# A block's preparation rebuilt, and D/2 added to the score tile by GpSimd instead of by matmuls

## The chip, the cores and the metric

The kernel runs on one core of one Trainium2 chip, in one launch. The metric is the time of that launch on the device, in microseconds. The core has five engines that matter here: TensorE (PE; its weight loads are PEld), VectorE (DVE), ScalarE (ACT), GpSimd (POOL) and SyncE (SP), which only issues DMAs. TensorE runs at one of two clocks, 1.2 or 2.4 GHz, and the profile tells which was granted as a share of the full one.

## The reference, cut to what matters

The input is two images of 64 by 64 positions with 64 channels. Four stages each add to it; the last two hold four bidirectional "mamba2" blocks each, along rows and along columns in turn. There are thus eight blocks, one after another, and these are what the change touches:

```python
def _mamba2(x, Win, Wconv, bconv, dt_bias, A_log, D, gn_w, Wout):
    z = zxbcdt[..., :DIN]
    xBC = jax.nn.silu(_causal_conv(zxbcdt[..., DIN:DIN + CONVDIM], Wconv, bconv))
    dt = jax.nn.softplus(zxbcdt[..., -NHEADS:] + dt_bias)
    A = -jnp.exp(A_log)
    y = _ssd(xh, dt, A, Bm, Cm) + rev(_ssd(rev(xh), rev(dt), A, rev(Bm), rev(Cm)))
    y = y + D[None, None, :, None] * xh
    y = _rmsnorm(y.reshape(b, l, DIN) * jax.nn.silu(z), gn_w)
    return y @ Wout
```

Its input is `_rmsnorm(x)`, and its output is added to x. `_ssd` forms for every sequence, head and pair of positions the product of a score (C times B), a decay (an exponential of sums of dt times A) and dt, and multiplies the 64 by 64 matrix by the sequence's x. The two directions together are one matrix whose entry is score times the smaller of two exponents' exponential, and D is added on its diagonal.

## The kernel before, in words

The program is written by hand for each engine, with a semaphore for every hand-over (`pe.wait_ge(sg("mixed"), ...)` waits, `.then_inc` tells). Each engine runs its instructions in order. Tokens are kept as 128 partitions (2 images by 64 channels) by 4096 columns, in eight chunks or groups of 512. Eight calls of `call(m, n, d, c)` make the eight blocks, c from 0 to 7; d is 0 for one axis (then a group of 512 columns is read from Y with a stride) and 1 for the other.

A call has three parts.

**Preparation.** ACT squares Y (line 750), PE multiplies by a matrix of 1/64 to get the mean over channels on all 128 partitions (line 476), ACT takes Ln and Exp chunk by chunk (lines 753, 755), and DVE scales Y by it into XP (line 1150). From XP PE makes sixteen chunks of z (line 487; ACT's tanh at line 765 and DVE's multiplication at line 1168 finish them, over four banks) and the chunk of dt (line 495). DVE adds the bias (line 1155), ACT and DVE make the softplus (`softplus_exp`, lines 629 to 635, and `softplus`, line 1005 on), and DVE scans dt times A (line 1179). Four tiles F, E, P, Q of exponents are each split into three bf16 parts: F and E on GpSimd (lines 850 to 853), P and Q on DVE (lines 1160 to 1163). SP stores F's and E's parts to DRAM (line 272) and, group by group, loads rows of them (line 258) and rows of P and Q (line 263). The z chunks and this chain are interleaved on DVE.

**The loop of steps.** `for tau in range(FIRST, LAST)` is run by PE, ACT and DVE, and GpSimd loops over u. Each of the 64 steps u handles one position of the outer axis: PE makes two tiles of exponents (`decay_logs`, lines 550 and 554), ACT copies one out of PSUM (line 780), DVE takes the smaller (line 1249), ACT its exponential (line 774), GpSimd multiplies it by the scores (line 861), and PE multiplies the result with x (`y`, line 570). `y` has 16 matmuls in a step: eight by the constant `Dhalf` (D/2 on a diagonal), eight by the product tile. Around this, with a period of four steps, `project_x` (line 515), ACT's tanh of x (786), `gate_x` (two DVE operations, line 1201) and `gate_y` (line 1231) run; with a period of eight steps `project_bc` (528), `gate_b` and `gate_c` (1213, 1218), `scores` (536), `scale_scores` (1225), ACT's squares (801), `sum_squares` (581), ACT's Ln and Exp of the gate (806, 808), `project_out` (587) and `grow` (1237, 1240). `every(tau, period, offset, count)` fixes the step at which each is placed. DK has three buffers, MM two.

**Tail.** The last output group leaves the loop, and line 1259 tells the next call that Y is ready.

```python
                    for hd in range(2):
                        for by, first_ in ((Dhalf, True), (MM[u % 2], False)):
                            for h4 in range(4):
```

Of the kernel before, what the change touches and what calls it, by code (L numbers as in the profile page):

```python
# [13 lines left out]
ALU = mybir.AluOpType  # L14
ACT = mybir.ActivationFunctionType
# [22 lines left out]
              ("restart", 512), ("dec_rhs", 512), ("dec_lhs", 128), ("thirds", 3), ("two", 1), ("mask16", 16), ("maskbc", 16), ("ones", 128), ("eps6", 1), ("eps6x4", 1), ("eps5", 1),  # L38
# [23 lines left out]
def program(nc, x, consts, pool_sel, state_sel, l0w, l1w, callw, out):  # L62
    ctx = ExitStack()
    with ctx:  # L64
# [83 lines left out]
        tz = [SQ[:, 512 * i:512 * i + 512] for i in range(4)]  # L148
        DT, dte, dtr, dty = (O[:, 512 * i:512 * i + 512] for i in range(4))
        dA_, dF, dE, dL = (O[:, 2048 + 512 * i:2560 + 512 * i] for i in range(4))  # L150
        dP, dQ, rest_v, rest_p = (SQ[:, 2048 + 512 * i:2560 + 512 * i] for i in range(4))

# [53 lines left out]
        LAST, FIRST = L + 15, -9  # L206
# [19 lines left out]
        def _(sp):  # L226
# [11 lines left out]
            def call(m, n, d, c):  # L238
# [12 lines left out]
                def rows_of_decay(g):  # L251
# [3 lines left out]
                    for k, name in enumerate("PQ"):  # L255
                        for j in range(3):
                            r0 = 32 * k + 2 * j
                            sp.dma_start(RHS[g % 2][r0:r0 + 2, :], cols_dram[k, j, 16 * g:16 * g + 16, :].rearrange(
                                "(b h) n -> b (h n)", h=8)).then_inc(sg(f"decay_cols{g % 2}"), 16)
                            l0 = 32 * k + 6 + 8 * j  # L260
                            for b in range(NB):
# [3 lines left out]
                                    sg(f"decay_rows{g % 2}"), 16)  # L265

                rows_of_x(0)
                rows_of_x(1)
                sp.wait_ge(sg("split_p"), c + 1)
                for k, name in enumerate("FE"):  # L270
                    for j in range(3):
                        sp.dma_start(cols_dram[k, j], SPLIT[name][j]).then_inc(sg("decay_stored"), 16)
                sp.wait_ge(sg("split_v"), c + 1)
                sp.wait_ge(sg("decay_stored"), (c + 1) * 96)
                sp.wait_ge(sg("zeroed"), 1)
# [24 lines left out]
        def _(pe):  # L300
# [167 lines left out]
            def call(m, n, d, c):  # L468
# [5 lines left out]
                for ch in range(NCHUNK):  # L474
                    pe.wait_ge(sg("squared"), c * NCHUNK + (ch + 1))
                    mm(bank[ch], C("mean64"), SQ[:, BANK * ch:BANK * ch + BANK], start=True,
                       stop=True).then_inc(sg("norm_ms"), 1)
                pe.wait_ge(sg(f"block_weights_loaded{d}"), (m * 2 + n) * 16 + 16)

                def z(i):  # L480

                    if i >= 4:
                        pe.wait_ge(sg("z_ready"), c * 16 + (i - 3))
                    else:
                        pe.wait_ge(sg("norm_log"), c * NCHUNK + (i + 1))
                        pe.wait_ge(sg("normed"), c * NCHUNK + (i // 2 + 1))
                    mm(bank[i % 4], W(f"wz{i % 2}"), xn_group(i // 2), start=True, stop=True).then_inc(  # L487
                        sg("z_psum"), 1)
                for i in range(4):
                    z(i)  # L490
# [963 lines left out]
```

## Time and profile before

| what | value |
|---|---|
| median of 3 runs | 2945.92 us (2945.87 to 2956.25) |
| the profiled execution's own time | 2958.37 us |
| its span | 2956.6 us |
| TensorE's granted clock, mean | 0.855 |
| PE busy | 2222.7 us, 75% |
| VectorE busy | 1883.0 us, 64% |
| ScalarE busy | 1841.8 us, 62% |
| GpSimd busy | 1088.8 us, 37% |
| the eight calls | from about 902 us to 2934 us |

Busy times are unions of an engine's instructions. They overlap between engines, so they show how full an engine is and not what ends last. The time before 902 us belongs to the first two stages, which the change doesn't touch.

### The profile page before, as it was taken

What the parts mean: (1) busy time and instruction counts of PE and PEld (TensorE: products, weight loads), DVE (VectorE), ACT (ScalarE), POOL (GpSimd) and SP (SyncE); (2) the same over time, 40 slices, a digit from 0 to 9 for tenths busy, and PEclk for the clock granted to TensorE, in tenths of its full rate; (3) what the DMA queues carried; (4) which work ended last, traced back from release to release, by engine and by line L of the source; (5) the groups of instructions that cost most, each with busy time, mean ns of one, the idle gap of its engine ahead of it and who ended that gap; (6) DMA issues with size and microseconds to landing.
All of it is one profiled execution on the core that took longest, in us unless ns stands there. A gap on an engine that the chain in (4) does not pass through costs nothing. (4 is left out here: it accounts for less than half of the span.)

```text
span 2956.6 us, 64250 instructions
## 1 busy us (share of the span) xinstructions
PE 2222.7 (75%) x26182; PEld 1131.4 (38%) x26182; DVE 1883.0 (64%) x2667; ACT 1841.8 (62%) x2939; POOL 1088.8 (37%) x859
## 2 busy tenths in 40 slices
PE   4276776777774897798698679658968986986896
PEld 3022222222221553454255245325524542552553
DVE  2588888888886564664665565566556646666564
ACT  1266766767655666576576657557665764666674
POOL 0044444444442452344154244214414432451342
PEclk6588888888887898898799899779988988998897
DMA  4000000000001111110111011011101101110111
GB/s 132 0 0 1 0 1 0 1 0 0 1 0 27 36 34 26 35 35 13 40 42 25 26 46 34 14 30 42 25 26 42 36 15 40 35 23 26 36 35 30
DMA packets 96695, 74.50 MB, mean 25 GB/s; under 512 B 69392, under 2 KB 77584, under 8 KB 95120
## 3 DMA queue, kind: packets, MB, share of 16 engines
q1 hardware_dynamic: 96400, 70.39, 10.0%
q8 instruction: 206, 3.38, 0.5%
q14 instruction: 89, 0.73, 0.1%
HBM read 20.54 MB, written 8.39 MB: 10 GB/s over the span
## 5 line engine op out<-in xcount | busy, mean ns | idle before, releaser
L861 POOL TENSOR_TENSOR SQ<-SQ 128x512 f32<-128x512 f32 x344 | 449.0, 1307 | 623.9 <-PE bank L570 397.1
L826 POOL TENSOR_TENSOR Y<-Z 128x512 f32<-128x512 f32 x256 | 331.0, 1293 | 530.8 <-DVE Z L1065 297.6
L1249 DVE TENSOR_TENSOR SQ<-bank,O 128x512 f32<-128x512 f32 x344 | 237.2, 690 | 420.0 <-ACT O L780 322.6
L774 ACT ACTIVATE SQ<-SQ 128x512 f32<-128x512 f32 x344 | 215.3, 626 | 202.0 <-DVE SQ L1249 201.9
L780 ACT ACTIVATE O<-bank 128x512 f32<-128x512 f32 x512 | 298.3, 583 | 61.3 <-PE bank L550 59.6
L550 PE MATMUL bank<-SS,work 32*128 32x512 bf16 x512 | 205.3, 401 | 155.8 <-ACT O L780 143.0
L861 POOL TENSOR_TENSOR SQ<-O,SQ 128x512 f32<-128x512 f32 x168 | 221.4, 1318 | 245.4 <-PE bank L570 212.9
L1065 DVE TENSOR_TENSOR_SCAN Z<-bank,SS 128x512 f32<-128x512 f32 x256 | 311.0, 1215 | 0.5
L448 PE MATMUL bank<-Y,constants 128*128 128x512 f32 x512 | 295.2, 661 | 6.5 <-DVE bank L1073 4.8
L515 PE MATMUL bank<-folded_weights,work 128*64 128x128 f32 x4096 | 298.2, 292 | 0.0
L570 PE MATMUL bank<-folded_weights,work 128*32 128x64 f32 x8192 | 283.3, 228 | 13.4 <-POOL SQ L861 13.3
L570 PE MATMUL bank<-SQ,work 128*32 128x64 f32 x8192 | 272.1, 222 | 0.0
L515 PEld LDWEIGHTS bank<-folded_weights,work 128*64 128x64 f32 x4096 | 235.8, 145 | 83.0 <-issue 83.0
L570 PEld LDWEIGHTS bank<-folded_weights,work 128*32 128x32 f32 x8192 | 186.2, 111 | 208.5 <-issue 182.4
L487 PE MATMUL bank<-XP,block_weights 128*128 128x512 f32 x256 | 151.6, 713 | 116.0 <-DVE Z L1168 114.7
L1057 DVE TENSOR_TENSOR SS<-SS,bank 128x512 f32<-128x512 f32 x256 | 173.6, 683 | 82.6 <-PE bank L436 66.9
L1249 DVE TENSOR_TENSOR O<-bank,O 128x512 f32<-128x512 f32 x168 | 115.8, 689 | 167.3 <-ACT O L780 140.9
L554 PE MATMUL bank<-SS,work 32*128 32x512 bf16 x512 | 206.2, 403 | 0.0
L712 ACT ACTIVATE Z<-bank 128x512 f32<-128x512 f32 x256 | 150.9, 590 | 77.7 <-PE bank L440 76.3
L570 PEld LDWEIGHTS bank<-SQ,work 128*32 128x32 f32 x8192 | 196.1, 112 | 0.0
L1201 DVE SCALAR_TENSOR_TENSOR work<-SQ,bank 64x512 f32<-64x512 f32 x256 | 174.3, 681 | 2.3 <-ACT SQ L786 0.3
L440 PE MATMUL bank<-work,Z 96*128 96x512 bf16 x256 | 109.7, 429 | 86.9 <-ACT Z L712 86.6
(260 smaller groups left out, 4064.3 us busy)
## 6 DMA issues: line engine op xcount, KB each, us to landing
work<-XP SPq DMA_DIRECT2D x256, 134.0 KB, 2.4
work<-extra SPq DMA_DIRECT2D x768, 8.0 KB
decay_cols_kept<-extra SPq DMA_DIRECT2D x48, 128.0 KB, 1.8
SS<-decay_cols_kept SPq DMA_DIRECT2D x384, 16.0 KB
block_weights<-callw SPq DMA_DIRECT2D x8, 735.0 KB, 4.2
Z<-state_sel SPq DMA_DIRECT2D x1, 2048.0 KB, 13.2
out<-O SPq DMA_DIRECT2D x2, 1024.0 KB, 8.5
constants<-consts SPq DMA_DIRECT2D x1, 1267.5 KB, 5.9
```

The source lines that it names most:

```text
L448: mm(bank[7], ident, hc[ta % 4], start=(ta % S1 == 0), stop=(ta % S1 == S1 - 1), skip_group_check=True).then_inc(sg("s1_acc"), 1)
L515: last = mm(bank[3][64 * b:64 * b + 64, 128 * j:128 * j + 128], XS[(k // 2) % 2][b][:, PADL * q + at:PADL * q + at + L], w, start=False, s ...
L550: mm(bank[2], rows[32:64, :], cols[32:64, :, :], start=True, stop=True, tile_position=(32, 0)).then_inc(sg("decay_logs2"), 1)
L554: mm(bank[u % 2], rows[0:32, :], cols[0:32, :, :], start=True, stop=True, tile_position=(0, 0)).then_inc(sg("decay_logs1"), 1)
L570: last = mm(bank[4 + k % 2][32 * h4:32 * h4 + 32, a:a + 64], xs[:, 32 * h:32 * h + 32], by[:, 64 * h:64 * h + 64], start=first_, stop=not ...
L774: A(DK[u % 3], DK[u % 3], ACT.Exp).then_inc(sg("decay_ready"), 1)
L780: A(D2C[u % 2], bank[2], ACT.Copy).then_inc(sg("d2_copied"), 1)
L826: g.tensor_tensor(hc[t_ % 4], hs[t_ % 4], c_copy[t_ % 4], ALU.mult).then_inc(sg("s1_hc"), 1)
L861: g.tensor_tensor(MM[u % 2].rearrange("p (h l) -> p h l", l=L), DK[u % 3].rearrange("p (h l) -> p h l", l=L), GM[(u // 8) % 2][:, 64 * (u ...
L1065: v.tensor_tensor_scan(hs[t_ % 4], bank[2 + t_ % 2], dbu[t_ % 2], 0.0, ALU.mult, ALU.add).then_inc(sg("s1_h"), 1)
L1201: last = v.scalar_tensor_tensor(X2[k % 2].rearrange("p (n b e) -> p n b e", b=2, e=HP)[h, :, b, :], TX[h, :].rearrange("p (n e) -> p n e", ...
L1249: v.tensor_tensor(DK[u % 3], bank[u % 2], D2C[u % 2], ALU.min).then_inc(sg("decay_least"), 1)
```

## The change

Preparation. DVE squares every other group. The mean over channels is made with a matrix of only 32 columns (`mean2`, of which two matter), so that four groups share a bank, Ln and Exp are taken twice in place of eight times, and a matmul with K=32 (`widen`) spreads each group's scale over 128 partitions again. Only three of the sixteen z chunks are made before the loop; the other thirteen are placed in the loop at fixed steps (`Z_SLOTS`): on all three engines in the same step tau. dt's matmuls follow each pair of groups. DVE's folding of weights moves behind the start of the chain and behind dt. The softplus is one run of DVE operations. E is split by ACT (two casts) and DVE (two subtractions), F alone by GpSimd. SP waits for each of the four tiles by itself, and loads a group's rows of P and Q ahead of those from DRAM.

The step. DVE multiplies scores and decays; GpSimd adds `Dhalf` to the product in place; PE has eight matmuls in `y`. ACT copies the exponents ahead of its exponential. DVE adds the two halves of the squares, so `sum_squares` is one matmul; it, the gate, `project_out` and `grow` come one step later.

```diff
+        Z_SLOTS = {-8: (3, 4), -7: (5, 6), -6: (7,), -5: (8,), -3: (9,), -1: (10,), 1: (11,), 3: (12,), 5: (13,),
+                   7: (14,), 9: (15,)}
-        LAST, FIRST = L + 15, -9
+        LAST, FIRST = L + 16, -9
...
+                for g in range(NGROUP):
+                    pe.wait_ge(sg(f"squared{g % 2}"), c * 4 + g // 2 + 1)
+                    j = 32 * (g % 4)
+                    last = mm(bank[g // 4][j:j + 32, :], C("mean2"), SQ[:, BANK * g:BANK * g + BANK], start=True,
+                              stop=True, tile_position=(0, j), skip_group_check=True)
...
+                    mm(bank[wide[g]], C("widen")[j:j + 32, :], scale2[g // 4][j:j + 32, :], start=True, stop=True,
+                       tile_position=(j, 0)).then_inc(sg("norm_wide"), 1)
...
                 def z(i):
+                    t, to = z_place(i)
+                    if i >= 8:
+                        pe.wait_ge(sg("z_ready"), c * 16 + i)
+                    elif i >= 3:
+                        pe.wait_ge(sg("z_ready"), c * 16 + (i - 2))
...
                     for hd in range(2):
-                        for by, first_ in ((Dhalf, True), (MM[u % 2], False)):
-                            for h4 in range(4):
+                        for h4 in range(4):
...
                 def sum_squares(g):
-                    pe.wait_ge(sg("gated_squared"), c * 8 + g + 1)
+                    pe.wait_ge(sg("squares_added"), c * 8 + g + 1)
...
-                    for hd in range(2):
-                        last = mm(bank[7], C("ssum"), squares[hd], start=(hd == 0), stop=(hd == 1))
-                    last.then_inc(sg("squares_psum"), 1)
+                    mm(bank[7], C("ssum"), squares[0], start=True, stop=True).then_inc(sg("squares_psum"), 1)
...
+                    for i in Z_SLOTS.get(tau, ()):
+                        z(i)
...
-                    for offset, work_ in ((-8, project_bc), (-4, scores), (11, sum_squares), (13, project_out)):
+                    for offset, work_ in ((-8, project_bc), (-4, scores), (12, sum_squares), (14, project_out)):
...
+                act.wait_ge(sg("dt_bounded"), c + 1)
+                A(dL, dL, ACT.Ln).then_inc(sg("dL_ready"), 1)
+                for j, (src, ready) in enumerate(((dE, "dE_ready"), (rest_e, "rest_E"))):
+                    act.wait_ge(sg(ready), c + 1)
+                    A(SPLIT["E"][j], src, ACT.Copy).then_inc(sg("cast_E"), 1)
...
                 for u in range(L):
-                    if u % 8 == 0:
-                        pool.wait_ge(sg("gm_ready"), c * 8 + u // 8 + 1)
-                    pool.wait_ge(sg("decay_ready"), c * L + u + 1)
-                    if u >= 2:
-                        pool.wait_ge(sg("y_psum"), c * L + u - 1)
-                    g.tensor_tensor(MM[u % 2].rearrange("p (h l) -> p h l", l=L),
-                                    DK[u % 3].rearrange("p (h l) -> p h l", l=L),
-                                    GM[(u // 8) % 2][:, 64 * (u % 8):64 * (u % 8) + 64].unsqueeze(1).broadcast_to(
-                                        [128, 8, L]), ALU.mult).then_inc(sg("mixed"), 1)
+                    pool.wait_ge(sg("weighted"), c * L + u + 1)
+                    g.tensor_tensor(MM[u % 2], MM[u % 2], Dhalf, ALU.add).then_inc(sg("mixed"), 1)
...
+                def add_squares(g):
+                    dve.wait_ge(sg("gated_squared"), c * 8 + g + 1)
+                    v.tensor_tensor(squares[0], squares[0], squares[1], ALU.add).then_inc(sg("squares_added"), 1)
...
                         v.tensor_tensor(DK[u % 3], bank[u % 2], D2C[u % 2], ALU.min).then_inc(sg("decay_least"), 1)
+                    u = tau
+                    if 0 <= u < L:
+                        if u % 8 == 0:
+                            dve.wait_ge(sg("gm_ready"), c * 8 + u // 8 + 1)
+                        dve.wait_ge(sg("decay_ready"), c * L + u + 1)
+                        if u >= 2:
+                            dve.wait_ge(sg("y_psum"), c * L + u - 1)
+                        v.tensor_tensor(MM[u % 2].rearrange("p (h l) -> p h l", l=L),
+                                        DK[u % 3].rearrange("p (h l) -> p h l", l=L),
+                                        GM[(u // 8) % 2][:, 64 * (u % 8):64 * (u % 8) + 64].unsqueeze(1).broadcast_to(
+                                            [128, 8, L]), ALU.mult).then_inc(sg("weighted"), 1)
+                    for i in Z_SLOTS.get(tau, ()):
+                        gate_z(i)
...
-                    for offset, work_ in ((-6, gate_b), (-5, gate_c), (-2, scale_scores), (14, grow)):
+                    for offset, work_ in ((-6, gate_b), (-5, gate_c), (-2, scale_scores), (11, add_squares), (15, grow)):
```

## Rows read from the trace of the kernel before

**Rows 1.** Busy time by stretch: calls 1 and 2, preparation, loop, tail; columns PE to POOL.

```profile
1159.20:1223.60 64.40, 41.74 (x144) 16.59 (x146) 42.03 (x72) 33.48 (x54) 8.75 (x9) 0.81 0.17 45
1223.60:1391.10 167.50, 150.54 (x2908) 91.21 (x2904) 97.87 (x149) 120.14 (x197) 81.43 (x64) 0.95 0.14 30
1391.10:1404.90 13.80, 8.22 (x41) 2.84 (x40) 3.85 (x6) 6.52 (x8) 1.22 (x1) 0.63 0.01 2
1405.10:1473.60 68.50, 41.54 (x140) 15.57 (x142) 44.81 (x72) 37.06 (x54) 8.76 (x9) 0.81 0.16 43
1473.60:1647.70 174.10, 154.72 (x2912) 93.74 (x2908) 101.24 (x149) 120.16 (x197) 83.44 (x63) 0.93 0.14 29
```

**Rows 2.** Groups by line, 1305 to 1347 us: sixteen steps of call 1.

```profile
L861 POOL TENSOR_TENSOR SQ<-SQ 128x512 f32<-128x512 f32 x11 | 14.6, 1328 | 19.0 <-PE bank L570 17.2 <-ACT SQ L774 1.7
L780 ACT ACTIVATE O<-bank 128x512 f32<-128x512 f32 x16 | 9.3, 584 | 1.1 <-PE bank L550 1.0
...
L1249 DVE TENSOR_TENSOR SQ<-bank,O 128x512 f32<-128x512 f32 x10 | 6.9, 691 | 10.5 <-ACT O L780 7.6 <-issue 2.8
...
L570 PEld LDWEIGHTS bank<-folded_weights,work 128*32 128x32 f32 x240 | 5.4, 109 | 5.1 <-issue 4.8 <-POOL SQ L861 0.2
...
L581 PE MATMUL bank<-O,constants 128*128 128x512 f32 x8 | 4.0, 619 | 0.0
```

**Rows 3.** Timeline, DVE and POOL: two DVE operations in a row, and line 1240 beside GpSimd and alone.

```profile
1222.08 0.69 DVE L1249 TENSOR_TENSOR SQ<-bank,O 128x512 f32<-128x512 f32 x1 [3.19 <-ACT O L780]
...
1222.69 0.68 DVE L1225 TENSOR_TENSOR SQ<-bank,constants 128x512 f32<-128x512 f32 x1
...
1391.06 1.26 POOL L861 TENSOR_TENSOR SQ<-SQ 128x512 f32<-128x512 f32 x1 [0.66 <-ACT SQ L774]
1391.54 1.32 DVE L1240 TENSOR_TENSOR Y<-Y,O 128x512 f32<-128x512 f32 x1
...
1404.13 0.69 DVE L1240 TENSOR_TENSOR Y<-Y,O 128x512 f32<-128x512 f32 x1
```

**Rows 4.** Timeline of call 1: ACT's gate and the copy behind it.

```profile
1363.88 0.69 ACT L806 ACTIVATE O<-bank,constants 128x512 f32<-128x512 f32 x1
...
1364.59 1.28 ACT L808 ACT_TABLE_LOAD   x1
...
1365.88 0.63 ACT L808 ACTIVATE O<-O 128x512 f32<-128x512 f32 x1
...
1366.94 0.58 ACT L780 ACTIVATE O<-bank 128x512 f32<-128x512 f32 x1
...
1367.60 0.69 DVE L1249 TENSOR_TENSOR SQ<-bank,O 128x512 f32<-128x512 f32 x1 [4.74 <-ACT O L780]
```

**Rows 5.** Timeline of a preparation (call 1; the last row is of call 2).

```profile
1159.21 4.27 ACT L750 ACTIVATE SQ<-Y 128x512 f32<-128x512 f32 x8 [2.61 <-DVE small L1259]
...
1168.56 3.60 PE L487 MATMUL bank<-XP,block_weights 128*128 128x512 f32 x8
...
1173.43 0.76 DVE L1150 SCALAR_TENSOR_TENSOR XP<-Y,block_weights,O 128x512 f32<-128x512 f32 x1 [0.48 <-ACT O L755]
...
1177.71 0.75 DVE L1155 TENSOR_SCALAR O<-bank,block_weights 128x512 f32<-128x512 f32 x1 [3.53 <-PE bank L495]
...
1193.13 1.22 DVE L1179 TENSOR_TENSOR_SCAN O<-constants,O 128x512 f32<-128x512 f32 x1
...
1203.61 2.80 SPq L272 DMA_DIRECT2D decay_cols_kept<-extra  x6
...
1208.36 1.56 SPq L263 DMA_DIRECT2D work<-extra  x2
...
1220.97 0.37 PE L550 MATMUL bank<-SS,work 32*128 32x512 bf16 x1 [1.46 <-DMA work<-extra]
...
1223.58 1.27 POOL L861 TENSOR_TENSOR SQ<-SQ 128x512 f32<-128x512 f32 x1 [19.99 <-ACT SQ L774]
...
1405.04 7.90 ACT L750 ACTIVATE SQ<-Y 128x512 f32<-128x512 f32 x8 [2.06 <-DVE small L1259]
```

More of the change, by code:

```diff
@@ L473, in W @@
                     return raw[:, a:b]
[L474 to L477, printed above, removed]
+                for g in range(NGROUP):
[3 more added lines that the diff above has]
+                              stop=True, tile_position=(0, j), skip_group_check=True)
+                    if g % 4 == 3:
+                        last.then_inc(sg("norm_ms"), 1)
@@ L498, in call @@
                 last.then_inc(sg("dt_psum"), 1)
-                for i in range(4, 16):
+                for i in range(3):
                     z(i)
@@ L748, in call @@
                 act.wait_ge(sg("y_ready"), y_value(m, n, d))
-                for g, at in enumerate(chunks):
-                    A(grid(SQ[:, at]), group_of(Y3, d, g), ACT.Square).then_inc(sg("squared"), 1)
-                for ch, at in enumerate(chunks):
-                    act.wait_ge(sg("norm_ms"), c * NCHUNK + (ch + 1))
-                    A(O[:, at], bank[ch], ACT.Ln, bias=C("eps6")).then_inc(sg("norm_log"), 1)
-                    act.wait_ge(sg("norm_log"), c * NCHUNK + (ch + 1))
-                    A(O[:, at], O[:, at], ACT.Exp, scale=-0.5).then_inc(sg("norm_scale"), 1)
@@ new lines, in call @@
+                for half in range(2):
+                    act.wait_ge(sg("norm_ms"), c * 2 + half + 1)
+                    A(scale2[half], bank[half], ACT.Ln, bias=C("eps6")).then_inc(sg("norm_log"), 1)
+                    act.wait_ge(sg("norm_log"), c * 2 + half + 1)
+                    A(scale2[half], scale2[half], ACT.Exp, scale=-0.5).then_inc(sg("norm_scale"), 1)
+                softplus_exp("dt", DT, dte, dtr, c)
+                act.wait_ge(sg("dt_bounded"), c + 1)
+                A(dL, dL, ACT.Ln).then_inc(sg("dL_ready"), 1)
@@ L767, in call @@
+                for i in range(3):
+                    z(i)
                 act.wait_ge(sg("folded"), c + 1)
-                act.wait_ge(sg("z_ready"), c * 16 + 16)
                 for tau in range(FIRST, LAST):
-                    u = tau + 1
-                    if 0 <= u < L:
-                        act.wait_ge(sg("decay_least"), c * L + u + 1)
-                        A(DK[u % 3], DK[u % 3], ACT.Exp).then_inc(sg("decay_ready"), 1)
                     u = tau + 2
@@ L802, in call @@
                         last.then_inc(sg("gated_squared"), 1)
[L803 removed]
+                    g = every(tau, 8, 13, NGROUP)
                     if g is not None:
```

211 lines of the change are left out of this document (116 added, 95 removed).

## The prediction

> **What bounds the kernel now.** I read first the busy time by stretch. A call falls into a preparation (64.4 us in call 1, 68.5 in call 2), a loop from GpSimd's first product to its last (167.5 and 174.1) and a tail of 13.8 [rows 1]. In the loop PE is busy 150.5 of 167.5 us, 90%, at 0.95 of its clock; ACT is busy 72%, DVE 58%, GpSimd 49%. So the loop is PE's, but not by much. The groups by line say the same from the other side: GpSimd's idle time ended mostly on PE's `y` (17.2 us of 16 steps) and VectorE's on ACT's copy [rows 2]. One stall is ACT's: Ln, a table load, Exp and what follows hold the copy of the exponents back by 3.1 us (1363.88 to 1366.94), and VectorE had then waited 4.74 us [rows 4]. Sixteen steps take about 42 us, so eight take 21.3 (167.5 / 63 x 8). In the preparation no engine is full (PE 65%, DVE 65%, ACT 52%): it is a chain. Its milestones in call 1, from the call's start at 1159.2: last scaled chunk done 15.0, dt's bias 18.5, scan 33.9, stores of the split tiles 44.4, loads of P and Q 49.2, first exponents 61.8, first product 64.4 [rows 5].
>
> **The loop, part by part.** PE loses the weight loads and matmuls of `Dhalf`: their loads fill 5.4 us of sixteen steps, and half of line 581's 4.0 goes too, so 3.7 us per eight steps [rows 2]. By that alone eight steps would take 17.6. What gets the work is VectorE and its partner. VectorE issues an operation on 512 columns every 0.61 us [rows 3]. Its operations in eight steps: 8 minima, 8 products (new), 4 of `gate_x`, 2 of `gate_y`, 2 and 1 of `gate_b` and `gate_c`, 1 scaling, 2 of `grow`, 1 `add_squares` (new): 29, or 17.7 us. That is no more than PE.
>
> But the product reads two tiles in SBUF, and so does GpSimd's addition. Line 1240, also of two SBUF inputs, takes 0.69 alone; begun 0.48 into a GpSimd operation of 1.26 it took 1.32, and it ended 0.54 after that one's end [rows 3]. The minimum, with one input in PSUM, keeps 0.69 beside GpSimd [rows 2]. So product and addition exclude each other. The addition I price as GpSimd's product now, 1.26 to 1.33 [rows 2, 3]. Where nothing else lies between two products, a step is 0.54 + 0.08 (a hand-over, 1367.52 to 1367.60 [rows 4]) + 1.26 = 1.88 us; steps 0 to 1, 4 to 5 and 6 to 7 are of this kind. Where `gate_x` twice and `gate_y` lie between, five operations give 3.05 (twice); with `gate_b` twice, 2.44. Where the operation between is itself of two SBUF inputs (`add_squares`, line 1240), it first waits for the addition: 0.46 + 0.61 + 0.69 + 0.08 + 1.26 = 3.10 (twice). Sum: 5.64 + 6.10 + 2.44 + 6.20 = 20.4 us for eight steps. PE's work behind it fits.
>
> A rule of the Trainium skill would make this larger. SBUF — State Buffer, "Who interferes with whom", says that a VectorE instruction with two SBUF inputs and a GpSimd instruction that reads SBUF block each other for the whole instruction, whoever is first. The trace shows the block, but the blocked operation ended 0.54 after the other and not a full 0.69. By the page's wording a step of the first kind is 0.15 longer, five such waits in eight steps 0.75, and the total below would be some 48 us more.
>
> ACT's gate adds to the 20.4. PE reaches the sum of squares behind `scores` in the same step, ACT then needs 0.69 + 1.28 + 0.63 and its copy 0.58 [rows 4], and in my layout the copy comes 1.4 us after VectorE wants it: 21.8. The clock was 0.95 and 0.93, and with dips as now I add 0.5: 22.3 for direction 1. Line 1240 is longer in direction 0 (strided), 0.5 more. Bounds: below, 20.4 (nothing but the exclusion); above, 22.3 + 1.7 if the gate costs all of its 3.1.
>
> **z in the loop.** A chunk costs PE 0.90 (3.60 for four [rows 5]). From tau = 1 to 9 five chunks stand in the loop, each made, tanh'ed and gated in the same tau. PE may take it up only after `y(tau - 1)`, so after the last addition: exponents and `y` 0.65, z 0.90, tanh 0.6, hand-overs. VectorE, in order, waits some 1.75 us for that and spends 0.61: 2.35 each, less where GpSimd's addition would have held it anyway; 11.2 in all. What doesn't exist yet in the first eight steps (first `gate_y`, `add_squares`, `grow`, ACT's gate) saves 5.2. So the loop is 25.6 + 24.2 + 5 x 22.3 + 19.4 (seven steps) = 180.7 in direction 1 and 184.5 in direction 0: 13 and 10.4 more than now. Bounds of the z stalls: 5 x 0.61 = 3 if other waits hide them, 14 if not.
>
> **The preparation.** Squares: ACT took 4.27 for eight (7.90 in direction 0) [rows 5]; four on each engine end at 2.5 (4.8). Two Ln and two Exp replace eight pairs, which paced the scaling at 1.24 (the last scaled chunk began at 14.2). I put the first scale at 4.2 and the last scaled chunk at 10.8. `mean2` and `widen` have no row like them; the nearest is line 487's 0.90 for 512 columns, and at the lower clock twice that, so both together 1.8 to 3.6 on this path; I take the middle. dt in PSUM about 2.2 later, bias 13.8, four ACT operations 16.7, eight softplus operations without z between them 22.2, scan done 24.3. It is done at 35.1 now (1193.13 + 1.22): 10.8 won. Then the splits: 14 operations on VectorE, half of them beside GpSimd's split of F, and two folding operations: 11.5, so `folded` at 35.8. SP's queue: six stores 2.8 (the last three start at about 31, when E is split), twelve row loads at 0.78, six loads from DRAM at about the 0.47 of a store; rows landed at about 46, against 61.8 now [rows 5].
>
> **What is late next** is not the rows. PE waits for `folded` before its first z of the loop part, and z(3) to z(8), `project_bc`, tanh, `gate_b`, `gate_c` and `scores` form one chain over three in-order engines: six chunks at 0.90 (the first ones at half clock, as PE idled before), about 3 for `project_bc`, 2.6 for tanh and bias, 2.4 for the gates, 2 for `scores`, and a hand-over each: 16.5. First exponents at 52.5. Then z(9), `gate_x`, scaling and z(10) stand on VectorE before the first product; first addition at 61.2, not 2.6 but 8.7 behind. So 16 us won at the rows become 3 in direction 1 and, as ACT's strided squares are halved, 5 in direction 0. Folding hidden behind the chain is priced at nothing; if its cover were gone it would be 2.6. Constants grow by 160 columns: under 1 us once, beside other loads.
>
> **Tail.** One matmul in place of two at the half clock saves 1.9, the addition costs 0.6 and a hand-over: 1.3 to 1.5 less.
>
> **Sum.** A pair of calls: preparation -8, loop +23.4, tail -3: +12.4. Four pairs: +50 us on the profiled execution's 2958.4. The median of the runs is 12.5 lower, so I forecast 2996.
>
> **Rivals.**
> (1) The forecast: exclusion and lockstep, +50. For it: rows 3. Chance 0.46.
> (2) Clock. In the tail, where PE waits, the clock is 0.63, in the preparation 0.81, in the full loop 0.95 [rows 1]. PE would be busy 75% of a loop step instead of 90%, with pauses for each addition. At 0.8 its 17.6 becomes 22 and every burst lands later: 1.3 us more per eight steps, 80 in all: 3075. TensorE: Matmul & The Clock Gate, "HAM oscillation", of the Trainium skill says that pauses between bursts let the clock fall back again and again; the rows above agree as far as tail and preparation go. Chance 0.14.
> (3) The other side, in the preparation: the lockstep chain is looser than I laid it out. If the first addition follows the rows' landing as now (46 + 8 = 54, so 10 won), ACT's gate hides (20.4 for eight steps) and z stalls cost half, the loop is 166 and a call is 13 us shorter: -105, 2840. It decides from about 21 us for eight steps. For it: PE gets 3.7 us per eight steps, and DVE's count is only 17.7. Against: the exclusion leaves 20.4 as a floor. Chance 0.27.
> (4) Gains and losses cancel, within 0.5% (15 us; about what a measurement of this kernel can tell from no change): 0.13.
> That `Dhalf`'s matmuls don't leave is excluded by the code.
>
> **Numbers.** Slower by over 0.5%: 0.46 + 0.14 = 0.60; within: 0.13; faster: 0.27. The range reaches to (2) and close to (3): 2850 to 3075. The likeliest case's own range, from its bounds of 20.4 to 24 us and the z stalls, is 2930 to 3075.
>
> **What would show it.** Right: starts of GpSimd's additions 1.9 us apart at the closest and 22 us per eight; VectorE's product taking 1.3 us and more in three of eight steps; the first addition 61 us after the call's start though the rows landed at 46; PE idle before `y`, waiting on GpSimd; VectorE idle before z's gates in the loop. Wrong: eight steps in under 21 us, products of 0.69 throughout, or a first addition before 56.

## The result, and the profile after

The changed kernel takes 3275.32 us (median of 4 runs, 3261.96 to 3278.11) against 2945.89; the ratio is 1.1104 with a 95% interval of 1.1076 to 1.1132. It is slower, as forecast, by 329 us and not by 50. The profiled execution took 3278.11 us, its span is 3276.3, and TensorE's mean clock fell from 0.855 to 0.757. Medians are of all executions and ratios of the undisturbed ones alone (in e5_z_early two of four ran slower than that, in e10_warm one of twelve), so the two need not agree exactly.

From the page of the changed kernel, busy times and some of the costliest groups of the step (line 888 is GpSimd's addition, 1294 VectorE's product, 591 `y`, 536 `project_x`; further down 806 is the copy, 571 the exponents, 512 the z chunks):

```profile
span 3276.3 us, 48402 instructions
PE 2330.2 (71%) x17990; PEld 1116.6 (34%) x17990; DVE 2333.8 (71%) x3291; ACT 1748.3 (53%) x2811; POOL 1039.5 (32%) x827
...
PEclk6588888888877776767777777678767977777766
...
L888 POOL TENSOR_TENSOR SQ<-SQ,folded_weights 128x512 f32<-128x512 f32 x512 | 652.9, 1275 | 1321.9 <-DVE SQ L1294 1321.9
...
L591 PE MATMUL bank<-SQ,work 128*32 128x64 f32 x8192 | 259.9, 256 | 208.9 <-POOL SQ L888 207.5
L536 PE MATMUL bank<-folded_weights,work 128*64 128x128 f32 x4096 | 375.9, 342 | 0.0
...
L1294 DVE TENSOR_TENSOR SQ<-SQ 128x512 f32<-128x512 f32 x344 | 261.5, 760 | 13.9 <-ACT SQ L810 13.9
```

PE has 8192 matmuls fewer in `y` alone, and yet is busy for 2330.2 us, 107.5 more than before: `project_x`, which the change leaves alone, went from a mean of 292 to 342 ns: it ran more often at the lower clock. PE's idle time before `y` ended on GpSimd (207.5 us).

The same stretches as in [rows 1], call 1 (preparation, loop, tail) and call 2 (preparation, loop); the columns are those of [rows 1], with the granted clock in the third place from the end:

```profile
1199.20:1267.50 68.30, 42.09 (x184) 17.34 (x188) 43.73 (x76) 22.04 (x37) 4.77 (x4) 0.68 0.17 45
1267.50:1483.60 216.10, 177.01 (x1849) 95.96 (x1842) 150.24 (x221) 120.67 (x198) 80.41 (x63) 0.70 0.10 22
1483.60:1497.10 13.50, 7.88 (x40) 2.27 (x38) 4.08 (x7) 6.52 (x8) 1.26 (x1) 0.69 0.00 0
1497.20:1565.90 68.70, 40.64 (x188) 14.79 (x192) 49.17 (x78) 24.31 (x38) 4.78 (x5) 0.80 0.17 45
1565.90:1775.10 209.20, 165.49 (x1841) 90.50 (x1834) 155.27 (x221) 120.48 (x197) 80.31 (x63) 0.77 0.11 23
```

In call 1 the preparation is 3.9 longer and the loop 48.6; in call 2 the preparation is the same and the loop 35.1 longer. So the time went into the loop, and there the clock is 0.70 and 0.77 where it was 0.95 and 0.93. Over all eight calls the loop, from GpSimd's first operation to its last, went from 171.2 to 209.8 us on average. Three stretches of eight steps show how the clock enters, two of call 1 and one of call 5:

```profile
1383.60:1412.70 29.10, 25.32 (x254) 14.23 (x250) 19.58 (x29) 16.04 (x27) 10.19 (x9) 0.65 0.13 27
1412.70:1438.20 25.50, 20.91 (x252) 11.56 (x248) 19.92 (x29) 15.93 (x27) 10.16 (x8) 0.80 0.14 31
2546.30:2570.30 24.00, 18.82 (x256) 10.22 (x252) 19.55 (x29) 15.98 (x27) 10.19 (x9) 0.93 0.15 33
```

The work is the same in all three (the 29 VectorE operations of the forecast), DVE, ACT and POOL are busy equally long, and only PE's time grows as its clock falls: 18.8, 20.9, 25.3 us, and the stretch with it: 24.0, 25.5, 29.1.

The starts of GpSimd's additions tell which steps grow. In groups 3 to 7 of all eight calls (a group is eight steps; the first two hold the z chunks) six of the eight spacings are the same at every clock: 1.9 us three times, 3.22 twice, 2.58 once. The other two are the step with ACT's gate, 4.55 to 8.06 us, and the step with `grow`, 4.66 to 6.71. All that the clock costs there falls on these two.

The timeline of the middle stretch has both (call 1; cut to the rows that matter):

```profile
1422.41 2.49 PE L557 MATMUL bank<-extra,work 64*128 64x64 f32 x16
...
1424.29 1.15 DVE L1294 TENSOR_TENSOR SQ<-SQ 128x512 f32<-128x512 f32 x1
1424.83 2.07 PE L603 MATMUL bank<-O,constants 128*128 128x512 f32 x2
...
1426.94 0.69 ACT L838 ACTIVATE O<-bank,constants 128x512 f32<-128x512 f32 x1 [2.01 <-PE bank L603]
...
1429.48 0.58 ACT L806 ACTIVATE O<-bank 128x512 f32<-128x512 f32 x1
...
1430.15 0.69 DVE L1286 TENSOR_TENSOR SQ<-bank,O 128x512 f32<-128x512 f32 x1 [2.69 <-issue]
...
1432.98 2.46 PE L608 MATMUL bank<-Z,folded_weights 128*128 128x512 f32 x4
...
1435.48 0.69 DVE L1274 TENSOR_TENSOR O<-bank,O 128x512 f32<-128x512 f32 x1 [2.14 <-PE bank L608]
```

Scores and the sum of squares (lines 557 and 603) slow down, ACT's gate waits 2.01 for them with the copy behind it, and VectorE's minimum, idle for 2.69, starts 0.09 after the copy's end; two steps on `grow` waits 2.14 for `project_out`. These are two in-order chains through PE that the low clock stretches. They answer to [rows 4], where VectorE waited 4.74 for the same gate while PE had other work.

### The profile page after: what moved, and what is told of

It is laid out like the page before. It is cut to its first block, busy times and chain, and to the rows that moved or that the text cites. A ratio compares the mean times of both kernels' runs of the same rounds, so it can differ in the third digit from the quotient of the medians.

```text
span 3276.3 us, 48402 instructions
## 1 busy us (share of the span) xinstructions
PE 2330.2 (71%) x17990; PEld 1116.6 (34%) x17990; DVE 2333.8 (71%) x3291; ACT 1748.3 (53%) x2811; POOL 1039.5 (32%) x827
## 4 chain that ended last, share of the span: by engine, by line
PE 46%; DVE 26%; ACT 13%; issue 9%; POOL 5%; DMA 0%; DVEq 0%; ACTq 0%; SPq 0%; POOLq 0%
PE bank L536 7%; PE bank L608 6%; PE bank L557 4%; PE bank L512 4%; DVE Z L1089 4%; POOL SQ L888 4%; PE bank L571 4%; PE bank L591 3%; PE bank L549 3%; PE bank L603 3%; DVE SQ L1294 2%; PE bank L463 2%; ACT O L806 2%; DVE SS L1081 1%; DVE SQ L1286 1%
## 5 line engine op out<-in xcount | busy, mean ns | idle before, releaser
L888 POOL TENSOR_TENSOR SQ<-SQ,folded_weights 128x512 f32<-128x512 f32 x512 | 652.9, 1275 | 1321.9 <-DVE SQ L1294 1321.9
L806 ACT ACTIVATE O<-bank 128x512 f32<-128x512 f32 x512 | 303.2, 592 | 394.8 <-PE bank L571 390.7
L591 PE MATMUL bank<-SQ,work 128*32 128x64 f32 x8192 | 259.9, 256 | 208.9 <-POOL SQ L888 207.5
L536 PE MATMUL bank<-folded_weights,work 128*64 128x128 f32 x4096 | 375.9, 342 | 0.0
L536 PEld LDWEIGHTS bank<-folded_weights,work 128*64 128x64 f32 x4096 | 296.8, 174 | 132.5 <-issue 132.5
L591 PEld LDWEIGHTS bank<-SQ,work 128*32 128x32 f32 x8192 | 166.5, 127 | 501.9 <-POOL SQ L888 273.5
L571 PE MATMUL bank<-SS,work 32*128 32x512 bf16 x512 | 235.2, 459 | 125.7 <-ACT O L806 125.7
L1294 DVE TENSOR_TENSOR SQ<-SQ 128x512 f32<-128x512 f32 x344 | 261.5, 760 | 13.9 <-ACT SQ L810 13.9
L1220 DVE SCALAR_TENSOR_TENSOR Z<-O,bank 128x512 f32<-128x512 f32 x128 | 86.4, 684 | 227.0 <-ACT O L794 227.0
L794 ACT ACTIVATE O<-bank 128x512 f32<-128x512 f32 x128 | 74.6, 597 | 315.6 <-PE bank L512 315.6
L575 PE MATMUL bank<-SS,work 32*128 32x512 bf16 x512 | 235.3, 459 | 0.0
L608 PE MATMUL bank<-Z,folded_weights 128*128 128x512 f32 x256 | 216.6, 995 | 6.2 <-ACT O L838 6.2
L1274 DVE TENSOR_TENSOR O<-bank,O 128x512 f32<-128x512 f32 x64 | 44.3, 692 | 191.8 <-PE bank L608 191.8
```

Of the source, the lines that this page charges most:

```text
L536: last = mm(bank[3][64 * b:64 * b + 64, 128 * j:128 * j + 128], XS[(k // 2) % 2][b][:, PADL * q + at:PADL * q + at + L], w, start=False, s ...
L571: mm(bank[2], rows[32:64, :], cols[32:64, :, :], start=True, stop=True, tile_position=(32, 0)).then_inc(sg("decay_logs2"), 1)
L591: last = mm(bank[4 + k % 2][32 * h4:32 * h4 + 32, a:a + 64], xs[:, 32 * h:32 * h + 32], MM[u % 2][:, 64 * h:64 * h + 64], start=True, stop ...
L608: last = mm(bank[7], wog[hd], Z2[:, TOK * hd + BANK * g:TOK * hd + BANK * g + BANK], start=(hd == 0), stop=(hd == 1))
L806: A(D2C[u % 2], bank[2], ACT.Copy).then_inc(sg("d2_copied"), 1)
L888: g.tensor_tensor(MM[u % 2], MM[u % 2], Dhalf, ALU.add).then_inc(sg("mixed"), 1)
```

## The experiments

Ratios are to the kernel before, run in the same round, with their 95% interval. They are what is compared: the median of the kernel before itself was 2941.10, 2944.61 and 2954.68 us in the three rounds. One theory, C, is that PE's pauses for the additions pull its clock down and that this costs most; X is that exclusion and in-order chain do it and the clock is incidental; Z is that the z chunks in the loop do it.

**e3_pool_mul.** The step of before inside the changed kernel:

```diff
-                    pool.wait_ge(sg("weighted"), c * L + u + 1)
-                    g.tensor_tensor(MM[u % 2], MM[u % 2], Dhalf, ALU.add).then_inc(sg("mixed"), 1)
...
+                    pool.wait_ge(sg("decay_ready"), c * L + u + 1)
+                    if u >= 2:
+                        pool.wait_ge(sg("y_psum"), c * L + u - 1)
+                    g.tensor_tensor(MM[u % 2].rearrange("p (h l) -> p h l", l=L),
+                                    DK[u % 3].rearrange("p (h l) -> p h l", l=L),
+                                    GM[(u // 8) % 2][:, 64 * (u % 8):64 * (u % 8) + 64].unsqueeze(1).broadcast_to(
+                                        [128, 8, L]), ALU.mult).then_inc(sg("mixed"), 1)
```

and `y` with sixteen matmuls, VectorE without a product.

> The new preparation and the z chunks in the loop, with the step of before (GpSimd multiplies, eight constant matmuls). What it differs from before by is the preparation and z's place. Working of the prediction: first product 61 us after the call's start against 64.4 and 68.5, minus 4 us a call, tail minus 1.5, z's five lockstep chunks plus 5 to 11: between 2930 and 2990 us, no clear gain. If the prediction's account of the preparation was too kind by as much as the result was off (7 us a call), 3000 to 3040 us.

Measured: 2950.69 us, ratio 1.0024 (1.0007 to 1.0041). All of the change but the moved product and addition comes out within 0.5% of before: the new preparation with z in the loop, ACT's copy ahead of its exponential, and VectorE's addition of the squares. That the sum is nothing doesn't say that each part is (see e6_mul_zearly and the ladder). Its loop of call 1 takes 179.6 us at a clock of 0.91 (167.5 at 0.95 before), but eight steps clear of z and of a dip take 20.9.

**e4_step_only.** The step alone, in the kernel before:

```diff
-                        for by, first_ in ((Dhalf, True), (MM[u % 2], False)):
...
+                                      start=True, stop=True, tile_position=(0, 32 * h4),
...
+                    pool.wait_ge(sg("weighted"), c * L + u + 1)
+                    g.tensor_tensor(MM[u % 2], MM[u % 2], Dhalf, ALU.add).then_inc(sg("mixed"), 1)
...
+                        v.tensor_tensor(MM[u % 2].rearrange("p (h l) -> p h l", l=L),
+                                        DK[u % 3].rearrange("p (h l) -> p h l", l=L),
+                                        GM[(u // 8) % 2][:, 64 * (u % 8):64 * (u % 8) + 64].unsqueeze(1).broadcast_to(
+                                            [128, 8, L]), ALU.mult).then_inc(sg("weighted"), 1)
```

and ACT's copy ahead of its exponential.

> The preparation of before, with the new step alone (VectorE multiplies, GpSimd adds D/2, eight matmuls in y, ACT copies first); sum_squares keeps two matmuls. If the step is what costs, nearly all of the 330 us: eight steps at 24 to 27 us against 21.3, so 3150 to 3260 us. If the preparation and z's place cost as much as the step: 3050 to 3120 us.

Measured: 3193.22 us, ratio 1.0856 (1.0820 to 1.0892), clock 0.799. The step costs 0.086 of the 0.110. The other 0.025 comes with what this run leaves out: the new preparation, z's place and the addition of the squares.

**e2_pe_adds.** In the changed kernel PE adds D/2 again, GpSimd does nothing in a step, VectorE multiplies:

```diff
+                        for by, first_ in ((Dhalf, True), (MM[u % 2], False)):
...
+                                          start=first_, stop=not first_, tile_position=(0, 32 * h4),
...
-                for u in range(L):
-                    pool.wait_ge(sg("weighted"), c * L + u + 1)
-                    g.tensor_tensor(MM[u % 2], MM[u % 2], Dhalf, ALU.add).then_inc(sg("mixed"), 1)
```

> The changed kernel, but D/2 is added by eight matmuls again and GpSimd has nothing to do in the step; VectorE still multiplies and z stays in the loop. Theory X: product back to 0.69 us throughout, VectorE no longer held, eight steps 21 to 22.5 us, kernel 2960 to 3040 us. Theory C alone gives much the same by way of a clock over 0.9, so this run with e1_fill tells them apart: if e1_fill wins nothing and this one wins all, the clock is not it. Theory Z (the z chunks in lockstep are the cost): first two groups of eight stay at 30 us and the kernel over 3150 us.

Measured: 3036.49 us, ratio 1.0311 (1.0269 to 1.0354). The product takes 681 ns, eight steps at the full clock 21.5, as expected; others 23 to 24. Moving the product to VectorE, against e3, costs 0.029 by itself. At the full clock that is 0.6 us in eight steps (21.5 against 20.9); on average over groups 3 to 7 of all calls it is 1.2 (22.5 against 21.3), so about half comes with a lower clock. Why VectorE's product costs the 0.6 was not tried.

**e1_fill.** The changed kernel with the eight constant matmuls as dead work:

```diff
+                        for by, first_ in ((Dhalf, True), (MM[u % 2], False)):
...
-                                      xs[:, 32 * h:32 * h + 32], MM[u % 2][:, 64 * h:64 * h + 64],
+                                          xs[:, 32 * h:32 * h + 32], by[:, 64 * h:64 * h + 64],
...
+                                          start=True, stop=True, tile_position=(0, 32 * h4),
```

> The changed kernel, with the eight matmuls by Dhalf put back into y as dead work: the matmuls by the product tile start the bank anew and overwrite them, so the output is that of the changed kernel and PE only has more to do (about 2.5 us per eight steps at the full clock). Theory C (PE's pauses for each addition let its clock fall to the lower level for a third of the loop, and the scores, project_x and project_out at half speed are what lengthens the steps): the granted clock in the loop goes up from about 0.75 to over 0.9, eight steps fall from 26.7 us to 22 to 24, and the kernel takes 3040 to 3150 us. Theory X (the exclusion of product and addition and the in-order chain set the step, the clock is incidental): the additional work stands in the chain, 3275 to 3340 us.

Measured: 3173.67 us, ratio 1.0789 (1.0758 to 1.0820). More work on the engine that is said to be relieved, and 102 us less by the medians (0.032 of the ratio, 93 us). The windows of its call 1 (whole loop, and eight steps):

```profile
1248.50:1448.10 199.60, 163.76 (x2866) 96.80 (x2862) 149.56 (x222) 120.08 (x198) 80.44 (x64) 0.86 0.11 25
1358.40:1382.00 23.60, 20.18 (x380) 12.03 (x376) 19.87 (x29) 15.87 (x27) 10.18 (x8) 0.93 0.16 34
```

The clock in the loop is 0.86 in place of 0.70, the loop 199.6 in place of 216.1. The exclusion is untouched (the product still takes 750 and 776 ns in its two groups), and dead work can shorten nothing except through the clock, so this difference is the clock's. The kernel stayed 23 us above what C expected, and its clock below that of before. Its groups at the full clock, nearly half of groups 3 to 7, take 22.7 us, 23.1 in direction 0, and the average is 23.8. The changed kernel has none at the full clock and averages 26.5; the kernel before takes 21.3 and 21.9 at the full clock and 22.4 on average. So of the 4.1 us that such a group lost, an estimate puts about 1.3 on the step itself and about 2.8 on the clock. It takes e1_fill's groups for what the changed step needs at the full clock, though e1_fill gives PE more to do, so the clock's part is rather larger.

**e9_aside.** e2_pe_adds with a GpSimd addition that nothing in the step waits for:

```diff
+                for u in range(L):
+                    pool.wait_ge(sg("mixed"), c * L + u + 1)
...
+                    g.tensor_tensor(O[:, 3584:4096], Dhalf, Dhalf, ALU.add).then_inc(sg("aside"), 1)
```

> e2_pe_adds (VectorE multiplies, PE adds D/2) with a GpSimd addition in each step that nothing in the step waits for: it adds Dhalf to itself into a spare tile. It has the exclusion and not the chain through GpSimd, and PE is as full as in e2_pe_adds. If the exclusion by itself sets the step: products again 1.1 us in three of eight steps, eight steps 22 to 23 us, and most of the way from e2_pe_adds (3036) to e1_fill (3174): 3120 to 3170 us. If it is the chain (y waits for the addition): 3036 to 3070 us.

Measured: 3052.83 us, ratio 1.0368 (1.0331 to 1.0406). The product goes from 681 to 723 and 729 ns (two groups), eight steps from 21.5 to 21.7. So the exclusion by itself costs about 0.006, a difference of two ratios that is no larger than their intervals. The addition aside reads one tile twice and takes 1.04 us, not 1.27, so it excludes for less long than the one in the change; the rest of the way to e1_fill, 0.042, is that longer hold and the chain (`y` waits for the addition, and the exponents behind `y` on PE), and this run doesn't part these two.

**e8_no_dhalf.** The kernel before without the constant matmuls and with nothing in their place; D times x is left out.

```diff
-                        for by, first_ in ((Dhalf, True), (MM[u % 2], False)):
...
-                                          xs[:, 32 * h:32 * h + 32], by[:, 64 * h:64 * h + 64],
-                                          start=first_, stop=not first_, tile_position=(0, 32 * h4),
+                                      xs[:, 32 * h:32 * h + 32], MM[u % 2][:, 64 * h:64 * h + 64],
+                                      start=True, stop=True, tile_position=(0, 32 * h4),
```

> The kernel before with the eight constant matmuls of each step left out and nothing in their place (D times x is missing from the output): what the removal alone is worth. By the prediction's count PE has 2.7 us less in eight steps, of 21.3. If PE bounds the loop and its clock stays: 18.7 to 19.5 us for eight steps, 2780 to 2840 us. If the clock falls with the load (theory C): some groups get longer than now, clock in the loop below 0.9, 2880 to 2960 us.

Measured: 3031.45 us, ratio 1.0293 (1.0262 to 1.0324). PE has 8192 matmuls less, nothing is added to any engine, and the kernel is slower. The windows of its call 1 (whole loop, eight steps mostly at the full clock, the next eight), and one of the kernel before at the full clock:

```profile
1230.60:1410.20 179.60, 156.05 (x1904) 86.73 (x1900) 102.49 (x149) 121.23 (x197) 80.30 (x64) 0.83 0.13 27
1294.70:1316.00 21.30, 17.71 (x250) 10.35 (x250) 13.10 (x21) 15.94 (x26) 10.43 (x8) 0.96 0.17 37
1316.00:1339.50 23.50, 20.85 (x252) 11.67 (x251) 14.11 (x21) 16.15 (x26) 10.16 (x8) 0.86 0.16 33
```

```profile
1307.50:1328.70 21.20, 19.40 (x380) 11.95 (x378) 12.59 (x20) 15.42 (x26) 10.21 (x8) 1.00 0.17 37
```

Two things at once. Near the full clock eight steps take 21.3 with PE busy for 17.7 us, and they took 21.2 with PE busy for 19.4: at that clock the removed work was not on the path. And in the loop as a whole the clock is 0.83 where it was 0.95, so whole groups take 23.5 and the loop 179.6 in place of 167.5. The removal is a loss of 86 us, and the clock is the only thing that these rows show worse.

**e5_z_early and e6_mul_zearly.** All z chunks before step 0, in the changed kernel and in e3_pool_mul:

```diff
-        Z_SLOTS = {-8: (3, 4), -7: (5, 6), -6: (7,), -5: (8,), -3: (9,), -1: (10,), 1: (11,), 3: (12,), 5: (13,), 7: (14,), 9: (15,)}
+        Z_SLOTS = {-8: (3, 4), -7: (5, 6), -6: (7,), -5: (8, 9), -4: (10, 11, 12), -3: (13, 14), -2: (15,)}
```

> The changed kernel with all thirteen z chunks of the loop placed before step 0 (at tau -8 to -2) instead of up to tau 9. Theory Z (the lockstep chunks cost): the first two groups of eight fall from 31 and 31 us to about 23 and 26, the start gets longer by six chunks of about 1.6 us (PE 0.9 and a hand-over): 3215 to 3260 us. If the chunks in the loop were covered: 3270 to 3320 us.

> New preparation, step of before, and z before the loop: what e3_pool_mul has, with the chunks moved as in e5_z_early. If lockstep chunks cost 10 us a call in the loop and 6 to 8 before it: 2920 to 2940 us. If it is the same: 2945 to 2960 us.

Measured: 3271.47 us, ratio 1.1013 (1.0931 to 1.1096), a wide interval; the ratio is 3243 us against the 2944.61 of its round, inside what Z expected, so the total alone doesn't refute Z. And 2951.47 us, ratio 1.0016 (0.9994 to 1.0039), the same as e3. In e6 the first minimum comes 72.2 us after call 1's start (57.8 in e3) and the loop from first to last minimum takes 158.5 (175.8). What the chunks cost in the loop they cost before it. In e5 the first two groups do fall as Z said (20.6 and 25.0 on average, 30.0 and 29.9 in the changed kernel), and the time to the first minimum grows by nearly as much: from one call's first minimum to the next call's it is 292.2 us against 293.6, with 253.9 before. At most 0.009 of the 0.110 is z's place, so Z falls as an account of the 329 us.

e6 also splits what e3 left together. With all chunks ahead of the loop as before, the first minimum comes 9.2 us later after the call's start than in the kernel before (72.3 against 63.1, 76.4 against 67.3 in direction 0), and from there to the call's end it takes 9.9 us less (176.3 against 186.2 on average). So the new preparation costs, and something around the step pays it back.

**e12_two_sums.** e3 with VectorE's `add_squares` undone (two matmuls, the gate one step earlier):

```diff
-                    pe.wait_ge(sg("squares_added"), c * 8 + g + 1)
+                    pe.wait_ge(sg("gated_squared"), c * 8 + g + 1)
...
-                    mm(bank[7], C("ssum"), squares[0], start=True, stop=True).then_inc(sg("squares_psum"), 1)
+                    for hd in range(2):
+                        last = mm(bank[7], C("ssum"), squares[hd], start=(hd == 0), stop=(hd == 1))
+                    last.then_inc(sg("squares_psum"), 1)
```

> e3_pool_mul with VectorE's addition of the squares undone (two matmuls in sum_squares again, the gate one step earlier, as before). What this part of the change is worth: in the tail it costs about 1 us a call by the difference of the chains (11.8 against 10.8 us from the last gate_y to the end); in the loop, where PE bounds, 0.9 us more of matmuls in eight steps against one VectorE operation less: 2950 to 2980 us. If the fuller PE keeps its clock better: 2940 to 2950 us.

Measured: 2917.47 us, ratio 0.9897 (0.9868 to 0.9925); e3's was 1.0024, in another round. A miss, on the good side: giving PE the second matmul back, with the gate one step earlier, gains 0.013. Which of the two gains it was not tried. Eight steps at the full clock fall from 20.9 to 20.0.

**e10_warm and e11_warm_tail.** e3 with dead matmuls where PE stood idle in the preparation, and in e11 also in the tail:

```diff
+                for _ in range(18):
+                    mm(bank[6], ident, C("restart"), start=True, stop=True)
                 pe.wait_ge(sg("folded"), c + 1)
...
+                    if g == NGROUP - 1:
+                        for _ in range(3):
+                            mm(bank[6], ident, C("restart"), start=True, stop=True)
```

> e3_pool_mul (new preparation, step of before) with 18 dead matmuls of 512 columns into a free bank, behind z(2) in each preparation, where PE stood idle for some 20 us before folded. They compute nothing that is used. Theory C: the z chain before the first step then runs at the full clock, and the first groups of steps too; z(3) to z(8), project_bc and scores win 4 to 6 us a call: 2900 to 2925 us. If PE's clock doesn't matter there (the chain is ACT's, VectorE's and the hand-overs'): 2945 to 2960 us, or more if the dead matmuls outlast the idle time.

> e10_warm with three more dead matmuls ahead of the last sum of squares in each call, where PE waits for ScalarE. Theory C: that sum and the last project_out, 2.1 and 3.8 us at the lower clock, come down towards 1.1 and 2.0, so 1 to 2.5 us a call less than e10_warm: 8 to 20 us. Otherwise within 5 us of e10_warm.

Measured: 2946.30 us, 0.9985 (0.9967 to 1.0002), and 2937.72 us, 0.9947 (0.9930 to 0.9964). The first missed what C expected and decides nothing: the dead matmuls ended 5.35 us before z(3), and z(3) and z(4) ran at half clock again (3.75 us for the two). The second holds: the tail wins 0.0038, about 11 us.

**e13_best.** e12_two_sums with the dead matmuls of e11:

> e12_two_sums with the dead matmuls of e11_warm_tail: the sum of the three. If C holds and the addition of the squares is worth its 10 us: e11_warm_tail plus 5 to 25 us, still under before (2941 us): 2900 to 2935 us.

Measured: 2888.76 us, ratio 0.9787 (0.9762 to 0.9813), the fastest of all, 66 us below the 2954.68 of before in its round (63 by the ratio). Its loop of call 1, eight of its steps, and its tail:

```profile
1207.80:1375.10 167.30, 155.01 (x2882) 92.70 (x2878) 101.17 (x155) 122.22 (x202) 80.34 (x63) 0.96 0.13 29
1299.60:1319.60 20.00, 19.34 (x380) 11.94 (x378) 13.14 (x21) 15.93 (x26) 10.25 (x9) 1.00 0.19 40
```

```profile
1377.06 2.84 PE L603 MATMUL bank<-constants 128*128 128x512 f32 x6
...
1379.74 1.88 PE L610 MATMUL bank<-O,constants 128*128 128x512 f32 x4
...
1382.40 1.98 PE L616 MATMUL bank<-Z,folded_weights 128*128 128x512 f32 x4 [0.78 <-ACT O L846]
```

Line 603 is the dead work. The last sum (1.88, four matmuls) and the last output (1.98) run at the full clock; in the changed kernel's tail of call 1 the two matmuls of the sum took 2.08 and the output 3.74. With PE busy for 19.34 of 20.00 us these eight steps are near what PE needs, which those of before (19.40 of 21.20) were not.

**The ladder.** Over before, in steps of the ratio: new preparation and the rest around the step +0.002 (e3), product to VectorE +0.029 (e2), addition on GpSimd with PE kept as full +0.048 (e1), PE emptied +0.032 (the change). Together 0.110. The last entry is not all that the clock costs: e1, e2 and e3 have their own share of the lower clock.

The first entry hides two that cancel. If the parts add up, which no run tests, e4 puts 0.025 on preparation, z's place and the addition of the squares with its later gate; e12 puts 0.013 of it on the latter, which leaves 0.012 for preparation and z; and as e3 holds all of this and comes to 0.002, the order of ACT's copy and exponential, its only other difference, would be a gain of some 0.022.

## Why the prediction was right or wrong

**The sign and the side were right, the size was not**: +50 us forecast, +329 measured, outside the range (2850 to 3075).

**"So the loop is PE's": wrong.** It rested on 90% busy. e8_no_dhalf took 8 matmuls from each step and eight steps at a high clock stayed at 21.3 us. It also shortened PE's busy time by 1.7 us (19.4 to 17.7) and not by the 2.7 of weight loads that the working took off. What set the steps instead would be, by [rows 4], the chain of copy, minimum, exponential and gate; e12's 20.0 us with ACT's order changed fits that, and no run shows it alone. The forecast used PE's 17.6 only as a floor that isn't reached, so this did no harm to the number; but it carried rival (3).

**Exclusion, 20.4 us for eight steps: the mechanism right.** The additions start 1.9, 2.58 and 3.22 us apart where 1.88, 2.44 and 3.05 were worked out (0.5 more in six steps), and products of 1.15 us are there (1424.29). The rule of the Trainium skill in SBUF — State Buffer, "Who interferes with whom", that the one who comes later is blocked, agrees with them. Its wording of the whole instruction would make a step of the first kind 2.03 us, and these are 1.9. As a price by itself the exclusion is small: e9_aside against e2_pe_adds, 0.006 or some 17 us.

**22.3 us for eight steps: the step that failed, by its term for the clock.** The working had 21.8, and then "The clock was 0.95 and 0.93, and with dips as now I add 0.5". It took the clock of before for a kernel that gives PE less to do. Measured, the clock in the loop was 0.70 and 0.77, and groups 3 to 7 took 26.5 us on average over all calls. At the full clock the same step takes 22.7 to 23.1 in e1_fill, so 0.8 to 0.9 us was missing from the 21.8 (22.3 in direction 0), and the clock took about 3.6 in place of 0.5 (an estimate: e1_fill gives PE more to do).

Even the shortest groups, 24.0 at 0.93, are not free of it. Here `project_out` of such a group (call 5) ran at half clock after PE had waited for ACT's copy, and `grow` waited for it; below, the same place in e1_fill at the full clock:

```profile
2562.30 0.39 PE L571 MATMUL bank<-SS,work 32*128 32x512 bf16 x1 [1.40 <-ACT O L806]
...
2563.86 3.63 PE L608 MATMUL bank<-Z,folded_weights 128*128 128x512 f32 x4
...
2567.53 0.69 DVE L1274 TENSOR_TENSOR O<-bank,O 128x512 f32<-128x512 f32 x1 [2.01 <-PE bank L608]
```

```profile
1400.39 1.98 PE L609 MATMUL bank<-Z,folded_weights 128*128 128x512 f32 x4
...
1402.41 0.69 DVE L1275 TENSOR_TENSOR O<-bank,O 128x512 f32<-128x512 f32 x1 [0.36 <-PE bank L609]
```

The step with `grow` then takes 3.24 us in place of 4.66, close to the forecast's 3.10. Rival (2) named the mechanism, PE busy for less and paused in each step, but gave it 0.14 and 1.3 us per eight steps. e1_fill and e8_no_dhalf show it from both sides: filled, the clock rises from 0.70 to 0.86 and 93 to 102 us go; emptied, it falls from 0.95 to 0.83 and 86 us come. How far the clock would fall for a given amount of PE work no run lets one work out: the same work got 0.65, 0.80 and 0.93.

The loop, forecast at 180.7 and 184.5, took 209.8 on average: 27 us a call, some 218 of the 279 us that the forecast missed. Most of the rest is the preparation.

**z in the loop, 11.2 a call: right in kind.** VectorE waits for each chunk. In call 1 of e3 against e6 the stretch from first to last minimum, with five chunks more in it, is 17.3 longer and the start 14.4 shorter; over all calls the two are 14.0 and 14.7.

**The preparation: milestones right, gain wrong.** From the call's start, forecast and measured: scan done 24.3 and 25.2, `folded` 35.8 and 36.7, first exponents 52.5 and 55.2, first addition 61.2 and 68.3. The timeline of call 1 of the changed kernel:

```profile
1223.14 1.23 DVE L1183 TENSOR_TENSOR_SCAN O<-constants,O 128x512 f32<-128x512 f32 x1
...
1235.26 0.67 DVE L1211 SCALAR_TENSOR_TENSOR folded_weights<-block_weights,constants 128x512 f32<-128x512 f32 x1
...
1254.37 0.60 PE L571 MATMUL bank<-SS,work 32*128 32x512 bf16 x1
...
1254.90 2.08 PE L512 MATMUL bank<-XP,block_weights 128*128 128x512 f32 x2
...
1262.73 2.08 PE L512 MATMUL bank<-XP,block_weights 128*128 128x512 f32 x2
...
1267.50 1.29 POOL L888 TENSOR_TENSOR SQ<-SQ,folded_weights 128x512 f32<-128x512 f32 x1 [38.08 <-DVE SQ L1294]
```

The last leg is 13.1 and not 8.7: z(9) and z(10) took 2.08 each where the working had 0.90, PE having been given the lower clock again. The forecast priced only the first chunks at half clock. So 9.9 won at the scan (10.8 forecast) became 3.9 lost at the first addition, and the rows' landing was indeed not what was late: the last six loads were issued 44.7 us after the call's start (46 forecast for the landing).

**Tail: 1.3 to 1.5 less forecast, 0.3 measured.** In call 1 the chain from the last `gate_y` to the end went from 11.8 to 10.7. But from GpSimd's last operation, as in [rows 1], the tail went from 13.8 to 13.5: the last `gate_y` now stands behind a `grow` that waited 1.48 for `project_out` at half clock. And in the loop the addition of the squares, with its later gate, cost what e12 shows.

**Chances.** Rival (3) on the other side fell with its first condition, steps under 21 us. The range's upper end came from rival (2)'s 1.3 us, a number with no run behind it. The nearest row, a clock of 0.63 in the tail, turns PE's 17.6 into 27.9 us, which over 64 groups would have allowed a bound near 3350. The likeliest case's own range was also too narrow for its bounds: 20.4 and 24 us for eight steps give 2874 and 3105, not 2930 and 3075. And two groups of 22.3 with 11.2 for z and 5.2 saved are 50.6, where the sum has 25.6 and 24.2; that is 0.8 a call and changes nothing.

## What to carry to other kernels

An engine that is 90% busy need not be on the path: take the work away and look before building something in its place. On this kernel work taken from PE at each step, without making the step shorter, lowered its clock and made all its other work slower, so a change that relieves PE has to be priced at the lower clock too, and matmuls that wait on a chain through three engines are where that price is paid. Dead matmuls in front of a dependent one can be worth more than they cost: 0.0038 here, in the tail. And an average busy time hides which steps grow: here two of eight took all of it.

## What the runs showed that had not been expected

Leaving out 8192 matmuls and adding nothing made the kernel 2.9% slower (e8), and adding 8192 dead ones to the changed kernel made it 2.8% faster by the ratios (1.0789 against 1.1104). VectorE's and GpSimd's exclusion, so plain in single instructions (0.68 to 1.15 us), moved the kernel by 0.6%, hardly more than the noise, when nothing waited for GpSimd. And the change holds a part that pays, which the prediction gave no price: with two matmuls in the sum, e12 needs 20.0 us for eight steps at the full clock where before needed 21.2. What else differs between these two in a step is that ACT's copy stands ahead of its exponential; that this order is what pays was argued and not tried alone.
